# Conv stage and MLP as one block: the MLP's first tiles run inside the last conv batch's steps

## The chip, the cores and the metric

One NeuronCore of a Trainium2 chip. The metric is the device time of one launch in microseconds (us). Three runs of the kernel before are given, and one profiled execution.

## The reference, cut to what matters

Two layers over x of 4 batches by 512 tokens by 256 features. Layer 0 is attention and a mixture of 16 experts. Layer 1 is a gated convolution, an MLP and a mixture of two experts; this is the part that matters here:

```python
h = _rmsnorm(x)                                   # x is the modulated layernorm
x = x + _mamba_fallback(h, W_in, conv_w, conv_b, W_out)   # the gated conv
h = _rmsnorm(x)
m = jnp.einsum('bte,de->btd', jax.nn.relu(jnp.einsum('btd,ed->bte', h, W_mlp1)), W_mlp2)
return x + m
...
h = _layernorm(x, axis=-1) * (1 + cb) + sb
x = x + gb * _L1_ffn_ref(h, L1_ffn_gate_w, L1_ffn_w_gate, L1_ffn_w_up, L1_ffn_w_down)
```

## The kernel before, in words

The work is a row of blocks. Within a block each engine runs a program of its own, in an order that is written out, and engines wait for one another by semaphores; between blocks all engines wait for all. Two blocks touch the change: `gated_conv` (L1506) and `mlp_and_dispatch` (L1866).

Every float32 product is made of three matmuls of split numbers, (high, low), (low, high), (high, high), by the helper `split3` (L47, L48, L49). So a weight or an activation is first copied to a rounded high part (ScalarE) and then subtracted from itself to a low part (VectorE or GpSimd).

**The conv block** works on one batch of 512 tokens at a time, four batches (0 to 3), as a wavefront: `wavefront` takes pairs (lag, stage), goes through steps, and in each step calls every stage, in the order listed, on the batch step minus lag. Each engine has its own list (TensorE L1834, ScalarE L1694, VectorE L1779, GpSimd L1600). For one batch: combine layer 0's results, layernorm, RMS norm, transpose to columns (`columns(0)`), up-projection in four parts (`up`, PSUM banks 2 to 5), conv taps, silu and gate, down-projection in four parts (`down`, banks 6 and 7), eviction (`y_out`, L1610), transposes back (`rows`, L1831, banks 0 and 1), add to H (`add`, L1778), squares (L1680), variance (L1740), root on GpSimd (L1579), scaled rows (`rms(1)`, L1654), transposes (`columns(1)`, L1790), high part (`hi(1)`, L1691) and low part (`lo(1)`, L1755) into hT, which the MLP reads. In TensorE's steps the last ones are: step 5, down(0) and down(1) of batch 3, columns(1) of batch 2, down(2) and down(3) of batch 3, rows of batch 3; step 6, columns(1) of batch 3.

**The MLP block** takes for each batch eight tiles of 128 hidden features. Per tile: up (six matmuls of 512 columns into banks 0 to 3 in turn), relu to the high part on ScalarE (L1997), low part on VectorE (L2039), and down (six matmuls into banks 4 and 5), which TensorE runs two tiles behind. Banks 6 and 7 serve transposes and routing. The MLP's weights lie in eight tiles; at batch 0 each tile is split first, ScalarE L1991 and VectorE L2033, three ahead and then one per tile. Their load (L1481) is issued in the conv block already, into a buffer that layer 0's results had held. From batch 1 on, ScalarE and VectorE also split the experts' up weights (L2019, L2099), which SyncE's queue loads (L1959) once all low parts of the MLP's weights are done and after it has zeroed a DRAM table from a tile that GpSimd sets (L1951, L1964).

Memory on the left side is laid out in the order of allocation. The conv block's tiles are freed when it closes, and the tiles of the dispatch, of the up weights and of the MLP take the same places.

Of the kernel before, what the change touches and what calls it, by code (L numbers as in the profile page):

```python
# [13 lines left out]
P = 128  # L14
D = 256
# [25 lines left out]
def f32(ap):  # L41

    return ap.bitcast(F32)
# [1439 lines left out]

class ConvWeights:

    def __init__(self, k, c, w_in, w_out, taps, mlp_st):
# [5 lines left out]
        self.yg, self.gb = (mlp_st.rows, k.sb("c_yg", [P, L0_TOPK, TT, D], F32, c)), k.sb("c_gb", [P, B, D], F32, c)  # L1492
        self.tap = k.sb("c_tap", [P, IT, TAPS + 1], F32, c)
        self.rows = k.sb("c_rows", [P, B, 2 * D], F32, c)
        self.k, self.w_in, self.wo_in, self.rows_in = k, k.sem("c_w_in"), k.sem("c_wo_in"), k.sem("c_rows_in")
# [10 lines left out]
def gated_conv(k, d, H, hT, weights, mlp_w):  # L1506

    nc = k.nc
    with ExitStack() as c:
        n = lambda s: f"c_{s}"  # L1510
        wi_st, wo_st, tap, w_in, wo_in = weights.wi, weights.wo, weights.tap, weights.w_in, weights.wo_in
        wi_hi = k.sb(n("wi_hi"), [P, DM, 2 * INNER], F32R, c)
        wi_lo = k.sb(n("wi_lo"), [P, DM, 2 * INNER], F32R, c)
        wo_hi = k.sb(n("wo_hi"), [P, IT, D], F32R, c)
        wo_lo = k.sb(n("wo_lo"), [P, IT, D], F32R, c)
# [4 lines left out]
        ss, sq = k.sb(n("ss"), [P, 2, B, TT], F32, c), k.sb(n("sq"), [P, 2, TT, D], F32, c)  # L1520
        hn = k.sb(n("hn"), [P, 2, TT, D], F32, c)
        rhi, rlo = k.sb(n("rhi"), [P, 2, DM, T], F32R, c), k.sb(n("rlo"), [P, 2, DM, T], F32R, c)
        acc = k.sb(n("acc"), [P, 2, T], F32, c)
        sx, sz = k.sb(n("sx"), [P, 2, T], F32, c), k.sb(n("sz"), [P, 2, T], F32, c)
        yv, yf, yg = weights.yv, weights.yf, weights.yg
        yhi, ylo = k.sb(n("yhi"), [P, IT, T], F32R, c), k.sb(n("ylo"), [P, IT, T], F32R, c)
# [12 lines left out]
        block = c.enter_context(nc.Block())  # L1539

# [11 lines left out]
        @block.sync  # L1552
        def _(sp):
# [13 lines left out]
            mlp_w.load(sp)  # L1567

        @block.gpsimd
        def _(pool):  # L1570
# [23 lines left out]
            def split_y(e):  # L1594
                def stage(b):
# [5 lines left out]
                      (3, split_y(2)), (3, split_y(3)), (0, pair), (2, gate(0)), (1, root(IN)))  # L1601

        @block.scalar
        def _(act):
# [79 lines left out]
            def hi(i):  # L1684
                def stage(b):
                    for m in range(DM):
# [12 lines left out]
        @block.vector  # L1699
        def _(dve):  # L1700
            own = Chain(dve, own_dve)

            def combine(b):
# [837 lines left out]
```

## Time and profile before

| | us |
|---|---|
| runs: median of 3 (lowest, highest) | 1178.86 (1175.69, 1179.64) |
| profiled execution, device time | 1173.97 |
| its span | 1171.9 |
| TensorE, busy share of the span | 81% |
| VectorE, ScalarE, GpSimd | 63%, 56%, 39% |
| mean granted TensorE clock | 0.897 of full speed |

The profiled execution took 4.9 us less than the median of the three runs; 2.1 us of it lie outside the span. Times in the text are counted from the span's start. A granted clock of 1.00 is 2.4 GHz and 0.50 is 1.2 GHz; a stretch between is a mixture of the two.

### The profile page before, as it was taken

Reading aid. Unit: us, or ns where it says so; the run is one execution under the profiler, and the core shown is the slowest. Engines: PE = TensorE matmul, PEld = TensorE weight load, DVE = VectorE, ACT = ScalarE, POOL = GpSimd, SP = SyncE. Lnnn points to the kernel's source line nnn. Section 1 sums busy time; section 2 is a strip of 40 time slices with the busy share of each in tenths; the row PEclk is TensorE's granted clock in tenths of the full one; section 3 lists DMA queues with packets and bytes.
Section 4 is the critical chain, followed back from the end, with each engine's and each line's share of the span. In section 5 each row is a group of like instructions: output and inputs, shape, how many; then the busy total and the mean of one; then the engine's idle time right before and its main releaser. Section 6 shows DMA issues by size and latency. Waiting matters only on the chain. (4 is left out here: it accounts for less than half of the span.)

```text
span 1171.9 us, 21496 instructions
## 1 busy us (share of the span) xinstructions
PE 954.3 (81%) x5454; PEld 796.3 (68%) x5454; DVE 742.1 (63%) x1917; ACT 652.3 (56%) x1693; POOL 456.9 (39%) x637
## 2 busy tenths in 40 slices
PE   6671999999997767969999970689699974999992
PEld 2461788888886655758999960468487753888882
DVE  4870798999994676468555535996447773444444
ACT  3562898999993345458666642579533322333331
POOL 3373564666662177603444443576301121010000
PEclk9786898999998787979999995799899986999997
DMA  7066443343322522447343429310042203000004
GB/s 247 17 222 212 114 102 90 91 90 90 90 54 64 180 100 101 153 150 251 124 128 121 126 98 303 99 45 1 14 143 75 72 28 127 24 31 33 28 15 152
DMA packets 112107, 123.15 MB, mean 105 GB/s; under 512 B 46720, under 2 KB 85120, under 8 KB 111896
## 3 DMA queue, kind: packets, MB, share of 16 engines
q1 hardware_dynamic: 102584, 97.89, 28.4%
q0 software_dynamic: 8608, 23.20, 5.3%
q10 hardware_dynamic: 832, 1.05, 0.3%
q8 instruction: 40, 0.66, 0.2%
q14 instruction: 43, 0.35, 0.1%
HBM read 77.73 MB, written 44.35 MB: 104 GB/s over the span
## 5 line engine op out<-in xcount | busy, mean ns | idle before, releaser
L717 ACT ACTIVATE PR<-PS,nmax 128x128 f32<-128x128 f32 (+3 forms) x256 | 135.7, 553 | 9.7 <-DVE nmax L758 8.4
L758 DVE TENSOR_REDUCE nmax<-PS 128x1 f32<-128x128 f32 (+3 forms) x256 | 113.5, 481 | 42.4 <-PE PS L661 37.0
L635 POOL TENSOR_SCALAR PR<-PR,rinv 128x128 f32<-128x128 f32 (+3 forms) x256 | 132.3, 537 | 0.0
L1355 POOL DMA_INDIRECT r_results<-r_y,r_to x79 | 75.9, 961 | 111.8 <-DVE r_to L1410 76.8
L660 PE MATMUL PS<-K,Q 128*128 128x128 f32 (+3 forms) x256 | 84.6, 390 | 30.4 <-PEq L138 26.4
L766 DVE TENSOR_TENSOR PTlo<-PS,PThi 128x512 fp32r<-128x512 f32 (+1 forms) x192 | 103.0, 590 | 2.9 <-ACT PThi L727 2.9
L727 ACT ACTIVATE PThi<-PS 128x512 fp32r<-128x512 f32 (+1 forms) x192 | 97.0, 547 | 6.7 <-PE PS L673 6.7
L673 PE MATMUL PS<-ident,PR 128*128 128x128 f32 x640 | 86.7, 281 | 3.6 <-DVE PTlo L766 3.0
L689 PE MATMUL PS<-PThi,V 128*128 128x512 f32 (+3 forms) x256 | 85.3, 346 | 1.1 <-DVE PTlo L766 0.5
L2350 DVE TENSOR_TENSOR x_h<-PS,x_sg 128x256 f32<-128x256 f32 x68 | 28.9, 424 | 86.4 <-ACT x_sg L2304 86.4
L2304 ACT ACTIVATE x_sg<-PS 128x256 f32<-128x256 f32 x68 | 26.2, 385 | 95.2 <-PE PS L2444 95.2
L2279 POOL DMA_INDIRECT x_results<-x_y,x_to x17 | 16.4, 963 | 156.2 <-DVE x_to L2345 143.8
L689 PE MATMUL PS<-PTlo,V 128*128 128x512 f32 (+3 forms) x256 | 76.2, 323 | 0.0
L673 PEld LDWEIGHTS PS<-ident,PR 128*128 128x128 f32 x640 | 69.6, 143 | 9.6 <-DVE PTlo L766 5.5
L949 POOL DMA_INDIRECT r_sorted<-o_hrow,o_slots x64 | 64.8, 1012 | 28.7 <-issue 18.7
L1399 DVE TENSOR_TENSOR r_xlo<-PS,r_xhi 128x256 fp32r<-128x256 f32 x79 | 33.4, 423 | 65.6 <-ACT r_xhi L1370 61.2
L660 PEld LDWEIGHTS PS<-K,Q 128*128 128x128 f32 x256 | 51.7, 206 | 32.8 <-issue 30.0
L2442 PE MATMUL PS<-r_wlo,r_xhi 128*128 x158 | 59.7, 378 | 2.5 <-issue 2.0
L1370 ACT ACTIVATE r_xhi<-PS 128x256 fp32r<-128x256 f32 x79 | 30.4, 385 | 56.1 <-PE PS L2444 54.0
L661 PE MATMUL PS<-maskb,identb 128*128 128x128 bf16 x256 | 60.8, 238 | 0.0
L717 ACT ACTIVATION_READ_ACCUMULATOR PR<-PS,nmax 128x1 f32 x256 | 58.7, 229 | 0.0
L2428 PE MATMUL PS<-x_w,x_hhi 128*128 (+1 forms) x136 | 57.2, 437 | 1.8 <-DVE x_hlo L2354 1.7
(374 smaller groups left out, 3067.8 us busy)
## 6 DMA issues: line engine op xcount, KB each, us to landing
r_xg<-r_sorted SPq DMA_DIRECT2D x79, 129.0 KB
r_wst<-in_routed SPq DMA_DIRECT2D x16, 608.0 KB, 5.3
K<-k_parts SPq DMA_DIRECT2D x120, 64.0 KB, 1.8
v_parts<-vp SPq DMA_DIRECT2D x4, 1024.0 KB, 7.5
V<-v_parts SPq DMA_DIRECT2D x64, 64.0 KB, 2.1
mlp_st<-r_results SPq DMA_DIRECT2D x8, 512.0 KB, 7.9
c_yg<-r_results SPq DMA_DIRECT2D x8, 512.0 KB
mlp_st<-in_up SPq DMA_DIRECT2D x8, 512.0 KB, 3.7
```

The costliest lines, as they stand in the source:

```text
L635: pool.tensor_scalar(PR[:, e % 4, i, 0:w], PR[:, e % 4, i, 0:w], rinv[:, e % 4, i:i + 1], 1.0, ALU.mult, ALU.mult).then_inc(norm_done, 1)
L660: pe.matmul(k.PS[:, i, 0:w], Q4[u][:, s // 2, P * i:P * i + P], K4[u][:, s, 0:w], start=True, stop=False)
L661: pe.matmul(k.PS[:, i, w - P:w], k.identb[:], k.maskb[:], start=False, stop=True).then_inc(s_ready, 1)
L673: ins = pe.transpose(k.PS[:, 4 + bank, at % 512:at % 512 + P], PR[:, (e - TRANS) % 4, i, P * j:P * j + P], k.ident[:])
L689: ins = pe.matmul(O[:, P * j:T], V4[u][:, j, s, :], pt[:, ge % 2, PT_AT[j]:PT_AT[j] + w], start=(s == 0 and j == 0 and part == 0), stop=(s ...
L717: act.activation(PR[:, e % 4, i, 0:w], k.PS[:, i, 0:w], ACT.Exp, bias=nmax[:, e % 4, i:i + 1], accum_out=rsum[:, e % 4, i:i + 1]).then_inc ...
L727: act.activation(PThi[:, e % 2, at:at + w], k.PS[:, 4 + n, 0:w], ACT.Copy).then_inc(hi_done, 1)
L758: dve.tensor_reduce(nmax[:, e % 4, i:i + 1], k.PS[:, i, 0:P * (i + 1)], AX_X, ALU.max, negate=True).then_inc(max_done, 1)
L766: dve.tensor_tensor(PTlo[:, (e - LO) % 2, at:at + w], k.PS[:, 4 + n, 0:w], f32(PThi[:, (e - LO) % 2, at:at + w]), ALU.subtract).then_inc(l ...
L949: pool.indirect_dma_start(out=d.sorted, out_offset=bass.IndirectOffsetOnAxis(ap=slots[:, b * TT + t, choice:choice + 1], axis=0), in_=hrow ...
L1355: pool.indirect_dma_start(out=d.results, out_offset=bass.IndirectOffsetOnAxis(ap=to[:, i % TO_LANES:i % TO_LANES + 1], axis=0), in_=y[:, i ...
L2442: pe.matmul(out, x_hi, w_lo, start=first, stop=False)
```

## The change

Five parts.

1. There is one block. `gated_conv` no longer opens one, but returns its engine programs; `mlp_and_dispatch` writes its own as generators, which yield after every tile, and the conv programs take each a generator and advance it where the order says. After the last conv stage each engine runs its generator to the end.
2. On TensorE, four turns of the MLP (up 0; up 1; up 2 and down 0; up 3 and down 1) come in step 6 ahead of columns(1) of batch 3.
3. On ScalarE, weight tiles 0 to 3 are split in step 5 after silu_x(2) of batch 3, and tiles 4 to 7 at the end of step 5; relu tile 0 comes after y_out of batch 3, tile 1 after the squares of batch 3, tiles 2 and 3 after rms(1) of batch 3.
4. On VectorE, the low parts of all eight weight tiles come in a row at the end of step 6, after lo(1) of batch 2 and ahead of add of batch 3; low tiles 0 and 1 come after that add, then the variance of batch 3, low tiles 2 and 3, and lo(1) of batch 3.
5. The banks are renamed (tiles in 2 to 5, results in 6 and 7, transposes and routing in 0 and 1), the conv tiles are allocated in another order, so that the MLP's weight tiles fall on tiles that are free early, and waits on conv semaphores are added. SyncE and GpSimd run their whole conv part first, then wait for the last up-projection, then run the MLP's part.

```diff
@@ gated_conv, allocation order
-        wi_hi = k.sb(n("wi_hi"), [P, DM, 2 * INNER], F32R, c)
-        wi_lo = k.sb(n("wi_lo"), [P, DM, 2 * INNER], F32R, c)
         wo_hi = k.sb(n("wo_hi"), [P, IT, D], F32R, c)
         wo_lo = k.sb(n("wo_lo"), [P, IT, D], F32R, c)
+        sq = k.sb(n("sq"), [P, 2, TT, D], F32, c)
+        hn = k.sb(n("hn"), [P, 2, TT, D], F32, c)
...
+        weights.early(c)
+        wi_hi = k.sb(n("wi_hi"), [P, DM, 2 * INNER], F32R, c)
+        wi_lo = k.sb(n("wi_lo"), [P, DM, 2 * INNER], F32R, c)
...
@@ ScalarE
-            wavefront((2, first_tap(1)), (4, hi(1)), (1, squares(0)), (2, silu_x(0)), (3, y_out), (2, silu_z(1)), (2, split_y(0)), (2, silu_x(1)),
+            def go_on(n):
+                def stage(b):
+                    if b == B - 1:
+                        for _ in range(n):
+                            next(mlp)
+                return stage
+            wavefront((2, first_tap(1)), (4, hi(1)), (1, squares(0)), (2, silu_x(0)), (3, y_out), (3, go_on(1)), (2, silu_z(1)), (2, split_y(0)), (2, silu_x(1)),
                       (1, rms(0)), (2, first_tap(2)), (2, split_y(1)), (2, silu_z(2)), (2, first_tap(3)), (1, hi(0)), (1, split_out_weights), (2, silu_x(2)),
-                      (3, squares(1)), (2, split_y(2)), (2, silu_z(3)), (0, split_weights), (0, normalize), (2, silu_x(3)), (1, first_tap(0)),
-                      (3, rms(1)), (2, split_y(3)), (1, silu_z(0)))
+                      (2, go_on(1)), (3, squares(1)), (3, go_on(1)), (2, split_y(2)), (2, silu_z(3)), (0, split_weights), (0, normalize), (2, silu_x(3)), (1, first_tap(0)),
+                      (3, rms(1)), (3, go_on(2)), (2, split_y(3)), (2, go_on(1)), (1, silu_z(0)))
+            for _ in mlp:
+                pass
@@ VectorE
-            wavefront((4, add), (3, conv(2)), (1, stats_of), (2, lo(0)), (1, shift), (3, conv(3)), (4, rms_var(1)), (1, modulate),
-                      (2, conv(0)), (4, lo(1)), (2, conv(1)), (1, rms_var(0)), (1, split_weights), (0, combine))
+            wavefront((4, add), (4, go_on(2)), (3, conv(2)), (1, stats_of), (2, lo(0)), (1, shift), (3, conv(3)), (4, rms_var(1)), (4, go_on(2)),
+                      (1, modulate), (2, conv(0)), (4, lo(1)), (2, conv(1)), (1, rms_var(0)), (1, split_weights), (0, combine), (3, go_on(1)))
@@ TensorE
-            wavefront((2, down(0)), (2, down(1)), (1, up(0)), (1, up(1)), (3, columns(1)), (2, down(2)), (2, down(3)), (1, up(2)),
+            def go_on(b):
+                if b == B - 1:
+                    for _ in range(4):
+                        next(mlp)
+            wavefront((2, down(0)), (2, down(1)), (1, up(0)), (1, up(1)), (3, go_on), (3, columns(1)), (2, down(2)), (2, down(3)), (1, up(2)),
                       (2, rows), (1, up(3)), (0, columns(0)))
@@ mlp_and_dispatch
+        TILE, RESULT = (lambda i: k.PS[:, 2 + i % 4, :]), (lambda m: k.PS[:, 6 + m, :])
+        SIDE = lambda g: k.PS[:, g, :]
@@ its ScalarE program
-                split_weights(b, i, split)
...
+            act.wait_ge(conv.combined, B)
+            for half in range(2):
+                for i in range(half * MLP_T // 2, (half + 1) * MLP_T // 2):
+                    split(i)
+                yield
@@ its VectorE program
+            dve.wait_ge(conv.z_ready, B * IT)
+            for i in range(MLP_T):
+                split(i)
+            yield
@@ its TensorE program
                 if b == 0:
                     pe.wait_ge(wlo_done, i + 1)
+                    pe.wait_ge(conv.conv_done, B * IT)
+                    pe.wait_ge(conv.sz_done, B * IT)
+                if i == 0:
+                    pe.wait_ge(conv.hT_done, (b + 1) * DM)
@@ its SyncE and GpSimd programs
+            sp.wait_ge(conv.z_ready, B * IT)
             load_rows(0)
...
+            pool.wait_ge(conv.z_ready, B * IT)
             pool.memset(zero[:, 0:D + 1], 0.0).then_inc(zero_set, 1)
```

## Rows read from the trace of the kernel before

**Rows 1.** Busy time of each engine in three stretches around the seam

```profile
core 0: us, PE busy (x) PEld busy (x) DVE busy (x) ACT busy (x) POOL busy (x), PEclk, DMA share, GB/s
826.50:846.00 19.50, 8.35 (x37) 5.45 (x36) 4.92 (x10) 11.56 (x29) 6.47 (x11) 0.80 0.01 3
846.00:870.70 24.70, 24.70 (x97) 20.17 (x97) 12.02 (x17) 7.65 (x14) 0.00 (x0) 0.88 0.53 164
870.70:955.00 84.30, 79.58 (x389) 64.37 (x387) 57.86 (x129) 31.72 (x50) 10.99 (x11) 1.00 0.20 60
```

**Rows 2.** TensorE's timeline at the seam: start, us, line, what [idle before, releaser]

```profile
828.41 1.87 PE L1790 MATMUL PS<-ident,c_hn 128*128 128x128 f32 x8 [1.85 <-ACT c_hn L1654]
830.51 0.50 PE L47 MATMUL PS<-c_ylo,c_wo_hi 128*128 128x512 f32 x1 [0.23 <-POOL c_ylo L1598]
...
834.83 1.07 PE L1831 MATMUL PS<-ident,c_yf 128*128 128x128 f32 x8 [1.27 <-ACT c_yf L1610]
840.50 2.44 PE L1790 MATMUL PS<-ident,c_hn 128*128 128x128 f32 x8 [4.60 <-ACT c_hn L1654]
846.00 0.79 PE L47 MATMUL PS<-hT,m_whi 128*128 128x512 f32 x1 [3.07 <-DVE m_wlo L2033]
```

**Rows 3.** ScalarE's timeline at the seam

```profile
827.77 1.69 ACT L1654 ACTIVATE c_hn<-H,c_rs 128x256 f32<-128x256 f32 x4
...
833.60 1.09 ACT L1610 ACTIVATE c_yf<-PS 128x512 f32<-128x512 f32 x2 [2.64 <-PE PS L49]
...
839.85 1.71 ACT L1654 ACTIVATE c_hn<-H,c_rs 128x256 f32<-128x256 f32 x4 [1.32 <-POOL c_rs L1579]
...
844.60 1.67 ACT L1991 ACTIVATE m_whi<-mlp_st 128x512 fp32r<-128x512 f32 x3 [1.02 <-PEq L1509]
```

**Rows 4.** VectorE's timeline at the seam

```profile
830.51 1.29 DVE L1755 TENSOR_TENSOR hT<-PS,hT 128x512 fp32r<-128x512 f32 x2 [3.96 <-ACT hT L1691]
835.50 1.29 DVE L1778 TENSOR_TENSOR H<-PS,H 128x512 f32<-128x512 f32 x2 [3.70 <-PE PS L1831]
838.56 0.17 DVE L1740 TENSOR_SCALAR c_var<-c_ss 128x4 f32<-128x4 f32 x1 [1.77 <-ACT c_sq L1680]
...
845.26 1.89 DVE L2033 TENSOR_TENSOR m_wlo<-mlp_st,m_whi 128x512 fp32r<-128x512 f32 x3 [0.96 <-ACT m_whi L1991]
849.60 0.69 DVE L2039 SCALAR_TENSOR_TENSOR m_lo<-PS,m_hi 128x512 fp32r<-128x512 f32 x1 [2.45 <-ACT m_hi L1997]
```

**Rows 5.** GpSimd's timeline: the root of batch 3

```profile
838.81 1.01 POOL L1579 TENSOR_TENSOR c_rs<-c_var,mhalf 128x4 f32<-128x4 f32 x1 [7.10 <-DVE c_var L1740]
```

**Rows 6.** TensorE's timeline: first matmul of up 4, batch 0, and of up 0, batch 1

```profile
857.10 0.39 PE L47 MATMUL PS<-hT,m_whi 128*128 128x512 f32 x1
...
870.70 0.39 PE L47 MATMUL PS<-hT,m_whi 128*128 128x512 f32 x1
```

**Rows 7.** Short stretches around two falls of the clock (columns as in rows 1)

```profile
756.70:758.90 2.20, 0.06 (x2) 0.05 (x1) 2.13 (x3) 2.20 (x5) 1.47 (x1) 1.00 0.10 9
758.90:761.00 2.10, 2.10 (x6) 1.14 (x6) 2.06 (x6) 1.11 (x2) 0.24 (x1) 0.72 0.82 237
...
836.00:840.50 4.50, 0.00 (x0) 0.03 (x1) 0.96 (x3) 2.35 (x10) 1.01 (x1) 0.76 0.00 0
...
849.00:852.00 3.00, 3.00 (x8) 2.32 (x8) 1.29 (x2) 1.56 (x3) 0.00 (x0) 0.50 0.00 0
```

**Rows 8.** The up weights' path: SyncE's issue, ScalarE's first use, landing times of DMA issues

```profile
860.60 42.54 SPq L1959 DMA_DIRECT2D mlp_st<-in_up  x6
...
872.75 1.05 ACT L2019 ACTIVATE u_hi<-mlp_st 128x1024 fp32r<-128x1024 f32 x1
...
mlp_st<-in_up SPq DMA_DIRECT2D x8, 512.0 KB, 3.7
d_sorted<-m_h SPq DMA_DIRECT2D x1, 2193.0 KB, 11.4
```

**Rows 9.** VectorE's timeline: the last combine of the conv block

```profile
778.39 2.21 DVE L1715 TENSOR_TENSOR X<-X,c_yg 128x1024 f32<-128x1024 f32 x1
```

More of the change, by code:

```diff
@@ L1 @@
+from collections import namedtuple
 from contextlib import ExitStack
@@ L1567, in _, with gpsimd @@
             mlp_w.load(sp)
-        @block.gpsimd
-        def _(pool):
+            for _ in mlp:
+                pass
+        def gpsimd(pool, mlp):
             def pair(b):
@@ L1601, in _, with scalar @@
                       (3, split_y(2)), (3, split_y(3)), (0, pair), (2, gate(0)), (1, root(IN)))
-        @block.scalar
-        def _(act):
+            for _ in mlp:
+                pass
+        def scalar(act, mlp):
             def y_out(b):
@@ L1778, in add, with go_on, stage, tensor @@
                     dve.tensor_tensor(x, k.PS[:, g, :].rearrange("p (t d) -> p t d", t=2), x, ALU.add).then_inc(h_added, 1)
-            wavefront((4, add), (3, conv(2)), (1, stats_of), (2, lo(0)), (1, shift), (3, conv(3)), (4, rms_var(1)), (1, modulate),
-                      (2, conv(0)), (4, lo(1)), (2, conv(1)), (1, rms_var(0)), (1, split_weights), (0, combine))
-        @block.tensor
-        def _(pe):
+            def go_on(n):
+                def stage(b):
+                    if b == B - 1:
+                        for _ in range(n):
+                            next(mlp)
+                return stage
+            wavefront((4, add), (4, go_on(2)), (3, conv(2)), (1, stats_of), (2, lo(0)), (1, shift), (3, conv(3)), (4, rms_var(1)), (4, go_on(2)),
+                      (1, modulate), (2, conv(0)), (4, lo(1)), (2, conv(1)), (1, rms_var(0)), (1, split_weights), (0, combine), (3, go_on(1)))
+            for _ in mlp:
+                pass
+        def tensor(pe, mlp):
             def columns(i):
@@ L1863, in __init__, with mlp_and_dispatch @@
         self.done = k.sem("u_done")
-def mlp_and_dispatch(k, H, hT, weights, gate_w, d, up_w, up_d):
+def mlp_and_dispatch(k, conv, H, hT, weights, gate_w, d, up_w, up_d):
     nc = k.nc
@@ L1918, in interleave @@
                             stage(b - back)
-        def split_weights(b, i, split):
-            if b == 0:
-                for j in range(0 if i == 0 else i + 2, min(i + 3, MLP_T)):
-                    split(j)
+                    yield
         def up_part(at, stage):
@@ L1936, in up_tiles, with sync @@
             return ust[:, j % 2, :], up_w.hi[:, j // L1_CHUNKS, cols], up_w.lo[:, j // L1_CHUNKS, cols]
-        @block.sync
-        def _(sp):
+        def sync(sp):
             def load_rows(b):
@@ L1985, in _, with scalar @@
             wavefront((0, root), (0, scatter))
-        @block.scalar
-        def _(act):
+            yield
+        def scalar(act):
             def split(i):
@@ L2160, in rows @@
                     pe.wait_ge(slots_done, b)
+                else:
+                    pe.wait_ge(conv.hT_done, B * DM)
                 for g in range(2):
@@ L2196, in ranks, with _ @@
                     pe.matmul(total, k.onesb[:], d.count[:, NT - 1:NT], start=True, stop=True).then_inc(t_ready, 1)
-            interleave(up, (2, 2, ranks), (1, 3, rows), (1, 6, columns), (2, 0, gate),
-                       *((0, i + 2, down(i)) for i in range(MLP_T - 2)), (0, 7, down(MLP_T - 2)), (0, 7, down(MLP_T - 1)))
+            yield from interleave(up, (2, 2, ranks), (1, 3, rows), (1, 6, columns), (2, 0, gate),
+                                  *((0, i + 2, down(i)) for i in range(MLP_T - 2)), (0, 7, down(MLP_T - 2)), (0, 7, down(MLP_T - 1)))
+        block = c.enter_context(nc.Block())
+        @block.sync
+        def _(sp):
+            conv.sync(sp, sync(sp))
+        @block.gpsimd
+        def _(pool):
+            conv.gpsimd(pool, gpsimd(pool))
+        @block.scalar
+        def _(act):
+            conv.scalar(act, scalar(act))
+        @block.vector
+        def _(dve):
+            conv.vector(dve, vector(dve))
+        @block.tensor
+        def _(pe):
+            conv.tensor(pe, tensor(pe))
 def sorted_experts(k, d, up_w, down_d, out):
```

88 lines of the change are left out of this document (48 added, 40 removed).

## The prediction

> **What bounds the kernel now.** The busy time by stretches was read first, then each engine's timeline at the seam, then the clock. In 19.5 us around the seam TensorE is busy for 8.35 us and no other engine is full either, while in the MLP's batches 1 to 3 TensorE is busy for 79.6 of 84.3 us at a clock of 1.00 [rows 1]. So the MLP is bound by TensorE, and the seam by a chain of waits. TensorE's timeline shows the chain's gaps: 4.60 us until the scaled rows of batch 3, 3.07 us until the MLP's first low weights [rows 2]. The links between are add at 835.50, squares, variance at 838.56, root at 838.81, scaled rows at 839.85, transposes from 840.50 [rows 2 to 5]. Then high and low parts of hT, and the end of the block; ScalarE's first weight split comes at 844.60, 1.02 us late [rows 3], and up 0 starts at 846.00. The clock has fallen in the long gap (0.76 over 836 to 840.5) and is still 0.50 from 849 to 852 [rows 7]. Up 4 of batch 0 starts at 857.10 and batch 1 at 870.70 [rows 6]: 10 groups of six matmuls lie between, 1.36 us each, or 0.227 us a matmul.
>
> The measure of the change is thus when up 4 starts. The groups behind it are in the same order before and after, and ScalarE and VectorE need together some 1.3 us per tile (0.5 to 0.6 relu, 0.69 low part [rows 4]) where TensorE needs 2.7 us for an up and a down, so they keep pace.
>
> **Part by part, on a time axis of the kernel before.**
>
> *ScalarE, splits 0 to 3.* Three splits took 1.67 us [rows 3], 0.52 us each from start to start, so four take 2.1 us. ScalarE is full there: scaled rows of batch 2 start at 827.77 with no wait before them [rows 3]. All behind it moves by 2.1 us: these scaled rows to 829.9, columns(1) of batch 2 on TensorE from 828.41 to 830.5, down(2) of batch 3 from 830.51 to 832.6, y_out from 833.60 to 835.7, rows from 834.83 to 836.9, done at 838.0 [rows 2, 3]. This work has its waits met: the wait on all four combines is for one that ended at 780.6 [rows 9].
>
> *ScalarE, splits 4 to 7.* Another 2.1 us. They sit before hi(1) of batch 2 and so push lo(1) on VectorE from 830.51 by 4.2 us to 834.7, done at 836.0 [rows 4]. y_out, at 835.7, is not pushed further.
>
> *VectorE, the eight low weight parts.* Three took 1.89 us [rows 4], 0.61 us each from start to start: eight take 4.9 us, from 836.0 to 840.9. Add of batch 3 is queued behind them. Its data come at 835.50 + 2.1 = 837.6, but it starts at 840.9: 5.4 us later than before. Squares, variance, root, scaled rows and lo(1) all wait for it. This is the new bound of the seam.
>
> *TensorE meanwhile.* Up 0, 1 and 2 (4.1 us, banks free) run from 838.0 to 842.1. Down 0 needs low tile 0, which is behind add: 840.9 + 1.3 + 0.6 = 842.8. Down 0 and up 3 then run to 845.6, and down 1 to 847.1 once low tile 1 is there (below).
>
> *The chain of batch 3.* Before, from add's start to the scaled rows' start is 839.85 - 835.50 = 4.35 us [rows 3, 4]. Now relu tile 1 on ScalarE (0.5) and low tile 1 on VectorE (0.7) stand between the squares and the variance: 5.55 us. Scaled rows start at 840.9 + 5.55 = 846.5 and take 1.7 us [rows 3], to 848.2. The last five transposes, at the half rate 0.3 us apart (2.44 us for eight [rows 2]) and at the full rate about 0.12 (an estimate from 1.07 us for eight with the last one's own length in it [rows 2]), end at 848.9. Columns(1) is queued ahead of up 4, so up 4 starts at 848.9.
>
> *Edits at nothing.* The block's end (under 1 us [rows 3]) is in the old chain and goes with it. The renamed banks have the same number of turns. hi(1) and lo(1) of batch 3 and relu tiles 2 and 3 are covered by down 2 and up 5 (2.7 us); without that cover they would cost up to 1.7 us. On SyncE's queue nothing stands between the MLP weights' load and the new wait but that wait, and it is met when the last up-projection ends, which TensorE runs ahead of its gap at 826.56. GpSimd's memsets stand behind the root of batch 3, now near 846.5, so the zero fill of the table is issued near 846.9 and the up weights' loads right behind it, against 860.60 before [rows 8]. Taken one after another, 11.4 us for the fill and 3.7 us for the first load [rows 8] land at 862.0; ScalarE first needs it at 872.75 - 8.2 = 864.5 [rows 8]. Covered by 2.5 us at this pessimistic price.
>
> **Sum.** 857.10 - 848.9 = 8.2 us earlier, and all later work moves along, since batches 1 to 3 wait for nothing outside. The profiled execution's 1173.97 becomes 1165.8. It stood 4.9 us below the median of the runs; against that median, 1178.86, the forecast is 1170.7.
>
> **Bounds of what no row shows.** If VectorE's row of splits did not delay add (its earliest, 837.6), TensorE alone would bind: 838.0 + 6 groups of 1.37 us + 0.8 for the transposes is 847.0, a gain of 10.1 us. If the clock is low through the seam, the lower end is below. I stay with 8.2, since each link was seen at nearly that length.
>
> **The clock, for and against.** TensorE is now without work from 826.56 (828.41 less 1.85 [rows 2]) to 830.5, 3.9 us, then has transposes, and waits again until 832.6. In the trace a stretch of 2.2 us almost without work was followed by a fall from 1.00 to 0.72 in the next 2.1 us [rows 7], and 4.5 us by 0.76 within it [rows 7]; so a fall near 830 is more likely than not. After 846.00 the engine worked steadily and was at 0.50 until about 852 [rows 7]. If it is low to 839 it hides: down(2) and down(3), 12 matmuls at 0.43 us in place of 0.23, end 2.4 us later and rows near 840.8, still ahead of add's 840.9. Low until 845, nine or ten matmuls of the MLP are slow too and the gain is about 4.5 to 5; until 850 about 2. The Trainium skill, page "TensorE: Matmul & The Clock Gate", section "HAM oscillation — how this bites in real kernels", says that waits between short bursts can throttle the engine at each burst anew; by that rule the seam, which still has waits in it, would stay at half rate beyond one fall. The rows after 852 hold 1.00 through three batches [rows 1], so I give it the small chance below.
>
> **Rivals.**
> - *A low clock well into the MLP's first tiles* (until 845 to 850). For it: the new gap at 826.6 and the second at 830 to 832.6. Against: from 838 on TensorE has work almost without a break. Gain 2 to 5 us: 1174 to 1177.
> - *The gain is given back at the up weights.* If fill and loads land later than 864.5, ScalarE, which takes all in order, stops at L2019 with relu tile 0 done and tile 1 behind it. Each us later gives one back; all is gone at 872.7, 26 us after the issue, where my price is 15. For it: fill and loads now start together. Result 1171 to 1179.
> - *The change does not do what it says.* Were any of the added waits on a semaphore of the end of the conv part, up 0 would stay behind it. But the waits name the last conv taps, the last silu_z (which ScalarE runs ahead of the scaled rows at 827.77 [rows 3]), and batch 0's hT; none is late. Then 1178.9; I give it 1%.
> - *Slower: the half rate holds through the whole first batch.* The waits for low tile 0, low tile 1 and the scaled rows, about 0.7, 0.2 and 1 us, keep the clock at 1.2 GHz. Price: each further us at 0.50 costs about half a us. The gain is gone near 854, and 96 matmuls at 0.427 us in place of 0.227 would cost 19 us less the 2.8 us that the old kernel paid from 846 to 852: a loss of about 8 us, 1187.
>
> **Chances.** The forecast (1168.5 to 1172.5) 0.70; low clock until 845 or 850 0.15, two thirds of it a gain above 3.5 us; up weights late 0.07; nothing done 0.01; slower 0.07. About 0.3%, 3.5 us, is what a measurement of this kernel can tell from no change. So faster 0.80, same 0.13, slower 0.07. The range: low end, the gain of 10.1 us and 2 to 3 us for the scatter of the three runs, 1166.0; high end, the low clock to 850, 1176.8.
>
> **What would show it.** Right: up 0 near 838, ahead of columns(1) of batch 3; eight L2033 in a row before the last L1778, which starts near 841; up 4 near 849; batch 1 near 862.5; the span shorter by 8 us and every stage from batch 1 on of the same length. Wrong: a clock of 0.50 beyond 843; an idle time before L2019 or L1997 in batch 1 put down to a DMA; up 4 after 855; an MLP batch 1 to 3 longer than 28 us; or a conv stage before 823 that has changed at all, since nothing but places in memory is different there.

## The result and the profile after

| | median, us | lowest to highest | executions |
|---|---|---|---|
| changed kernel | 1164.43 | 1160.24 to 1168.03 | 4 |
| kernel before, on the same chip | 1177.28 | 1173.41 to 1179.64 | 4 |

The ratio is 0.9893 with a 95% interval of [0.9847, 0.9938]: faster by 1.1%, clear of the noise. The forecast was 1170.7 with a range from 1166.0 to 1176.8, so the result lies 6.3 us below the forecast and 1.6 us below the range. The profiled execution took 1168.03 us with a span of 1166.2.

The stretches of the changed kernel come first, to be held against [rows 1] and [rows 7]. Columns: from:to, length, busy time of PE, PEld, DVE, ACT, POOL with instructions, granted clock, DMA share, GB/s.

```profile
827.80:831.80 4.00, 0.00 (x0) 0.02 (x1) 0.17 (x1) 4.00 (x14) 1.46 (x2) 0.92 0.30 39
831.80:834.90 3.10, 3.09 (x10) 2.29 (x11) 0.00 (x0) 3.10 (x8) 3.10 (x3) 0.50 0.00 0
834.90:838.40 3.50, 3.50 (x10) 2.73 (x9) 2.42 (x5) 1.53 (x4) 0.19 (x1) 0.56 0.01 2
838.40:841.50 3.10, 1.83 (x13) 1.36 (x12) 3.10 (x7) 1.08 (x2) 0.00 (x0) 1.00 0.01 1
841.50:850.10 8.60, 8.60 (x44) 7.22 (x43) 3.60 (x7) 5.46 (x17) 1.65 (x7) 1.00 0.44 102
850.10:863.69 13.59, 13.59 (x61) 11.21 (x61) 7.16 (x10) 3.37 (x6) 0.00 (x0) 1.00 0.74 208
863.69:946.20 82.51, 77.92 (x377) 62.90 (x375) 57.85 (x128) 30.51 (x49) 10.97 (x11) 1.00 0.19 61
```

Before, TensorE did nothing for 4.60 us ahead of the last transposes and for 3.07 us ahead of the MLP's first tile [rows 2]; now it is full from 841.50 to 863.69. The clock fell in the gap that the change opened (0.92, then 0.50 and 0.56) and was back at 1.00 by 838.4; before, it was at 0.50 in the MLP's first tiles [rows 7], whose first 14 matmuls took 6.07 us (846.00 to 852.07); in the changed kernel they take 3.27. Next TensorE's timeline, against [rows 2] and [rows 6].

```profile
831.81 2.44 PE L1820 MATMUL PS<-ident,c_hn 128*128 128x128 f32 x8 [4.05 <-ACT c_hn L1668]
...
840.09 1.07 PE L1861 MATMUL PS<-ident,c_yf 128*128 128x128 f32 x8 [1.27 <-ACT c_yf L1624]
840.91 0.48 PE L48 MATMUL PS<-hT,m_whi 128*128 128x512 f32 x1
...
849.17 1.03 PE L1820 MATMUL PS<-ident,c_hn 128*128 128x128 f32 x8
849.96 0.48 PE L48 MATMUL PS<-hT,m_whi 128*128 128x512 f32 x1
...
863.69 0.39 PE L48 MATMUL PS<-hT,m_whi 128*128 128x512 f32 x1
```

Up 0 (840.91) follows the rows of batch 3 at once, and up 4 (849.96) follows columns(1) at once; neither has an idle time before it. ScalarE and VectorE, against [rows 3] and [rows 4]:

```profile
825.44 0.63 ACT L1677 ACTIVATE c_sx<-c_acc 128x512 f32<-128x512 f32 x1 [0.18 <-DVE c_acc L1790]
825.98 2.18 ACT L2027 ACTIVATE m_whi<-mlp_st 128x512 fp32r<-128x512 f32 x4
...
831.17 1.70 ACT L1668 ACTIVATE c_hn<-H,c_rs 128x256 f32<-128x256 f32 x4
...
833.29 2.18 ACT L2027 ACTIVATE m_whi<-mlp_st 128x512 fp32r<-128x512 f32 x4
...
847.43 1.71 ACT L1668 ACTIVATE c_hn<-H,c_rs 128x256 f32<-128x256 f32 x4 [1.92 <-POOL c_rs L1592]
...
865.75 1.05 ACT L2054 ACTIVATE u_hi<-mlp_st 128x1024 fp32r<-128x1024 f32 x1
```

```profile
835.99 1.29 DVE L1778 TENSOR_TENSOR hT<-PS,hT 128x512 fp32r<-128x512 f32 x2 [6.03 <-ACT hT L1705]
837.19 4.89 DVE L2072 TENSOR_TENSOR m_wlo<-mlp_st,m_whi 128x512 fp32r<-128x512 f32 x8
842.00 1.28 DVE L1801 TENSOR_TENSOR H<-PS,H 128x512 f32<-128x512 f32 x2
```

The row of eight low weights and the add right behind it without an idle time are what was forecast. For the up weights' path [rows 8], SyncE's issues and their landings (KB each, median us from issue to landing):

```profile
847.72 0.37 SPq L1986 DMA_DIRECT2D d_sorted<-m_h  x1
...
d_sorted<-m_h SPq DMA_DIRECT2D x1, 2193.0 KB, 10.8
mlp_st<-in_up SPq DMA_DIRECT2D x3, 512.0 KB, 10.4
```

Beside the fill, the first three loads take 10.4 us instead of 3.7, yet the first split of them on ScalarE (L2054, 865.75) waits for nothing.

**A measure for the seam.** Starting points drift by several us between executions, so all traces below are measured from the start of silu_x(2) of batch 3 on ScalarE (825.44 here, 824.12 before) to the first up matmul of batch 1 (863.69; before 870.70 [rows 6]). That is 46.58 us before and 38.25 after: 8.33 us less, where 8.2 was forecast. The seam is right and the total is not, so the experiments ask both what makes the seam's gain and where the other 4 us or so came from.

### The profile page after: what moved, and what is told of

It reads as the page before. It is cut to its first block and busy times, and to the rows that moved or that the text cites. A ratio compares the mean times of both kernels' runs of the same rounds, so it can differ in the third digit from the quotient of the medians.

```text
span 1166.2 us, 21505 instructions
## 1 busy us (share of the span) xinstructions
PE 951.9 (82%) x5454; PEld 795.4 (68%) x5454; DVE 742.0 (64%) x1917; ACT 650.6 (56%) x1693; POOL 454.6 (39%) x637
## 3 DMA queue, kind: packets, MB, share of 16 engines
q10 hardware_dynamic: 832, 1.05, 0.3%
```

## The experiments

Four series ran, each with fresh runs of the kernel before on its chip (medians 1175.81, 1173.27, 1173.83 and 1175.3, of 29, 11, 23 and 11 executions; all 74 together 1174.61). Ratios are against those. Offsets, written +x, count from silu_x(2) as above.

### Copies: how far the clock itself can be trusted

`null_before` and `null_before2` are the kernel before, `after_again`, `after_third` and `after_fourth` the changed kernel, without an edit.

> The kernel before against itself, unchanged. Both theories expect a ratio of 1 within its interval. What it measures is the scatter: how far two medians of a handful of runs of one kernel lie apart (the four runs known span 1173.4 to 1179.6), and how long each stretch of the trace is in a second execution. If stretches outside the seam differ by 1 us or more between two executions of this same kernel, the differences of that size between before and after outside the seam mean nothing.

> The kernel before once more, unchanged, for a third trace of it. silu_x of part 2, batch 3 starts at 824.1 and 828.8 in the two traces so far, and between 817.7 and 825.4 in the eight of kernels with the new order, of which 1.1 us are explained. If the rest is scatter between executions, this trace has a value between 819 and 829, with the difference in attention (227.9 to 233.4 us so far) and the experts; if something of the new kernels shortens the early stages, it is at 824 or above again.

> The changed kernel, once more, with more rounds. Measure: the seam, from the start of silu_x of part 2, batch 3, on ScalarE to the first up matmul of batch 1; 46.6 us in the trace before, 38.3 us in the trace after. Theory A (the change acts at the seam alone, and the first comparison's 12.9 us is 8.3 us and scatter): ratio near 0.993, 7 to 10 us; seam 38.3 again. Theory B (the new places in memory or the moved transfers also shorten other stages): ratio near 0.989, 12 to 14 us, and the stretches before 731 or after batch 1 of the MLP shorter than in the kernel before by 3 us or more in all.

> The changed kernel a third time, beside the others on the same chip. Theory A (sum of stages: 8.3 us at the seam, 0.9 at the conv block's start, 0.2 to 0.3 in the last conv batch): ratio 0.992, with an interval that may hold 0.990. Theory B (there is 3 us more elsewhere): 0.989 to 0.990.

> The changed kernel beside them. Seam 38.2 to 38.5 us as in three traces, ratio to the kernel before 0.990 to 0.993.

| kernel | median us (executions) | ratio [95%] | seam, us |
|---|---|---|---|
| null_before | 1174.4 (12) | 0.9988 [0.9971, 1.0006] | 45.13 |
| null_before2 | 1173.94 (12) | 1.0001 [0.9985, 1.0017] | 46.65 |
| after_again | 1164.01 (6) | 0.9901 [0.9876, 0.9926] | 38.00 |
| after_third | 1163.98 (5) | 0.9911 [0.9892, 0.993] | 38.00 |
| after_fourth | 1165.11 (6) | 0.9896 [0.9873, 0.9918] | 38.46 |

The 24 executions of the copies of before lie between 1170.83 and 1180.08, median 1173.94, mean 1174.5; the changed kernel's 21 have median 1164.40 and mean 1164.1. One execution scatters by about 2.2 us (standard deviation), far from the seam: in the three traces of before, attention from its first to its last Q matmul takes 230.35, 231.86 and 233.44 us, in the four of the changed kernel 227.92 to 231.75. The three runs on which the forecast was set, median 1178.86, stand 4.9 us above the copies' median. With the fresh runs and the first comparison's four there are 102 executions of the kernel before: 1170.35 to 1180.44, median 1174.6, mean 1174.9.

### one_block: the block's end alone

All turns of the MLP inside the conv stages are taken out; each generator runs whole after them.

```diff
@@ ScalarE
-            wavefront(... (3, y_out), (3, go_on(1)), (2, silu_z(1)), ...
+            wavefront(... (3, y_out), (2, silu_z(1)), ...
...
@@ VectorE
-            wavefront((4, add), (4, go_on(2)), (3, conv(2)), ...
+            wavefront((4, add), (3, conv(2)), ...
...
@@ TensorE
-            wavefront(... (1, up(1)), (3, go_on), (3, columns(1)), ...
+            wavefront(... (1, up(1)), (3, columns(1)), ...
```

> All of the change but the interleaving: one block, new memory layout, renamed banks, added waits; every turn of the MLP comes after the conv part on each engine. Theory A: only the end of the block goes, up 0 starts some 1.1 us earlier; seam 45.5 us, ratio 0.999. Theory B: the layout's share of the gain is here too, so 4 us or more beyond that, ratio 0.995 or less. A rival on the seam, that the end of the block was what cost, expects a seam near 40.

Measured: 1173.04 (12), ratio 0.9978 [0.9959, 0.9996], seam 45.89. The seam hardly differs from the 45.1 to 46.7 of the three traces of before, but the clock hides a part of it. In the stretch between the rows of batch 3 and up 0 the block's end can be seen by itself: 11.17 us in all three traces of before and in layout_only, 10.12 here, with a wait of 2.01 us ahead of up 0 in place of 3.07. So the block's end is worth 1.05 us, as expected; what hides it is that the rows came at +11.95, behind downs with six matmuls at half rate, where two of the three traces of before have them at +10.71 (the third at +12.07). One block is what makes the rest possible and one eighth of what saves the time. The ratio, 2.6 us with 2.1 either way, also holds the new places in memory (layout_only).

**The clock's share.** From up 0 on, the six traces without TensorE's turns differ only in how many of the MLP's first matmuls run at half rate. The first 14 took 6.07, 4.66 and 4.82 us in the three traces of before, 6.06 in layout_only, 5.23 here and 4.95 in splits_only; the rest up to batch 1 took 18.59 to 18.63 in all six. In all eleven traces with the turns they took 3.27 to 3.30. Before, the MLP starts behind waits of 4.60 and 3.07 us; with the turns it starts behind a wait of 1.27 us and a batch of transposes. So 1.4 to 2.8 us of the seam's gain are matmuls that run faster, and not idle time that is filled.

### splits_only: the weight splits moved, TensorE's turns left out

ScalarE's two turns of splits and VectorE's turn of eight stay where the change puts them; TensorE's four turns and the relu and low tiles go behind the conv part.

```diff
@@ ScalarE
- (3, y_out), (3, go_on(1)), (2, silu_z(1))
+ (3, y_out), (2, silu_z(1))
- (3, squares(1)), (3, go_on(1)), (2, split_y(2))
+ (3, squares(1)), (2, split_y(2))
- (3, rms(1)), (3, go_on(2)), (2, split_y(3))
+ (3, rms(1)), (2, split_y(3))
@@ VectorE
- (4, add), (4, go_on(2)), ...  (4, rms_var(1)), (4, go_on(2)),
+ (4, add), ...  (4, rms_var(1)),
@@ TensorE
- (1, up(1)), (3, go_on), (3, columns(1))
+ (1, up(1)), (3, columns(1))
```

> The changed kernel with the weight splits where the change puts them, but TensorE's first four turns and the relu and low tiles after the conv part. My theory of the prediction says that the splits alone cost: add of batch 3 starts 5.4 us later, columns(1) of batch 3 about 5 us later, up 0 near 848 instead of 846 and with the same slow clock, so a seam of 48 to 48.5 us, 1.5 to 2 us longer than before, ratio 1.001 to 1.002. The rival, that having the weights split ahead is what brings the gain, expects a seam of 43 us or less.

Measured: 1173.1 (10), ratio 0.9979 [0.9961, 0.9997], seam 47.18. A seam of 48 to 48.5 and a ratio above 1 had been expected; the seam is about 1 us shorter, and the ratio lies on the other side of 1, the new places in memory being in it too. TensorE's timeline:

```profile
842.37 2.44 PE L1820 MATMUL PS<-ident,c_hn 128*128 128x128 f32 x8 [6.96 <-ACT c_hn L1668]
844.45 0.77 PE L48 MATMUL PS<-hT,m_whi 128*128 128x512 f32 x1
```

VectorE's add of batch 3 is at +16.56, as in the changed kernel, so TensorE waits 6.96 us in place of 4.60 [rows 2] for the scaled rows. Up 0 follows the transposes without the 3.07 us wait of before; what the early splits save there is paid for ahead of the transposes. The last step from 47.18 to 38.25, 8.9 us, is therefore TensorE's four turns (with the relu and low tiles that feed them): they fill that wait, and with them the transposes of batch 3 (2.44 us here, 1.03 in the changed kernel) and the MLP's first 14 matmuls (4.95 and 3.27) run at full clock.

### warm_fill: is the clock's fall paid for?

Fourteen matmuls whose results nobody reads are put into TensorE's gap, behind down(1) of batch 3; nothing else changes.

```diff
+            def fill(b):
+                if b == B - 1:
+                    pe.wait_ge(conv_done, B * IT - 1)
+                    pe.wait_ge(sz_done, B * IT - 1)
+                    for _ in range(14):
+                        pe.matmul(k.PS[:, 2, :], wo_hi[:, 0, 0:P], yhi[:, 0, :], start=True, stop=True)
-            wavefront((2, down(0)), (2, down(1)), (1, up(0)), ...
+            wavefront((2, down(0)), (2, down(1)), (2, fill), (1, up(0)), ...
```

> The changed kernel with 14 matmuls of 512 columns into an idle PSUM bank (results unused) in TensorE's gap ahead of columns(1) of batch 2, where the changed kernel's trace has 4.05 us without work and the clock at 0.50 for the 12 matmuls of down(2) and down(3) of batch 3. Theory A (that fall hides behind VectorE's row of eight splits, as the prediction had it): down(2) and down(3) take 2.8 us instead of 4.3, rows of batch 3 start 1.5 to 2.4 us earlier, add still starts behind the splits, 16.6 us after silu_x(2); seam 38.3 us again, within 0.4. Rival (the clock is the bound there): seam 36 to 36.5.

Measured: 1164.09 (4), ratio 0.9922 [0.9895, 0.9949], seam 38.02. TensorE's timeline (silu_x(2) at 819.37), and then the stretches:

```profile
821.53 3.33 PE L1873 MATMUL PS<-c_yhi,c_wo_hi 128*128 128x512 f32 x14
...
832.16 1.07 PE L1861 MATMUL PS<-ident,c_yf 128*128 128x128 f32 x8 [1.27 <-ACT c_yf L1624]
```

```profile
822.00:826.00 4.00, 3.11 (x14) 2.19 (x12) 0.17 (x1) 4.00 (x15) 1.72 (x2) 1.00 0.11 23
826.00:829.00 3.00, 2.64 (x13) 1.78 (x13) 0.00 (x0) 3.00 (x8) 3.00 (x3) 1.00 0.01 3
```

The clock stays at 1.00 and the rows of batch 3 come at +12.79, not +14.65. The add is at +16.57 all the same, behind VectorE's row, and the seam with it. In the four traces of the changed kernel the clock over the 3 us from the transposes of batch 2 on is 0.50 to 0.53 each time, and 0.50 to 0.90 over the next 3 us; the rows come at +13.42 to +14.83 and the seam is 38.00 to 38.46. So the fall costs between nothing and 0.46 us: hidden nearly whole, as forecast.

### low_halves: VectorE's row cut in two

Low tiles 0 to 3 are split in a turn right after the variance of batch 2; tiles 4 to 7 only ahead of low tile 2.

```diff
- (4, rms_var(1)), (4, go_on(2)),
+ (4, rms_var(1)), (4, go_on(2)), (3, go_on(1)),
- (0, combine), (3, go_on(1)))
+ (0, combine))
...
-            for i in range(MLP_T):
+            for i in range(MLP_T // 2):
                 split(i)
             yield
...
+                if b == 0 and i == 2:
+                    for j in range(MLP_T // 2, MLP_T):
+                        split(j)
```

> The changed kernel with VectorE's row of eight low splits broken up: tiles 0 to 3 ahead of lo(1) of batch 2, where VectorE idles, tiles 4 to 7 after the variance of batch 3, ahead of low tile 2. The prediction's upper bound said 10.1 us instead of 8.2, a seam of 36.4, if this row did not delay add. With the slow clock seen at down(2) and down(3), my theory now is that TensorE binds at nearly the same length: rows of batch 3 at 14.7 us after silu_x(2), then 0.8 + 8.2 + 0.8 us of its own work: up 4 at 24.4, against 24.6 in the trace of the changed kernel. So add starts 1.2 us earlier and the seam is 38.0 to 38.3. The rival, VectorE's row alone is the bound, expects 36.4.

Measured: 1165.08 (4), ratio 0.993 [0.9902, 0.9958], seam 38.38. VectorE's timeline (silu_x(2) at 817.66):

```profile
822.09 3.58 DVE L2072 TENSOR_TENSOR m_wlo<-mlp_st,m_whi 128x512 fp32r<-128x512 f32 x4
...
833.08 1.29 DVE L1801 TENSOR_TENSOR H<-PS,H 128x512 f32<-128x512 f32 x2 [3.29 <-PE PS L1861]
...
838.29 2.49 DVE L2072 TENSOR_TENSOR m_wlo<-mlp_st,m_whi 128x512 fp32r<-128x512 f32 x4
```

The add is free of the row now: it waits 3.29 us for TensorE and is at +15.42, 1.1 us earlier. But the rows come at +14.76 and up 0 at +15.58, where the changed kernel has +14.65 and +15.47. TensorE holds the seam by itself here. The forecast's bound of 10.1 us for "TensorE alone" was wrong in just this: it had up 0 at 838.0, +13.9, with a clock that did not fall. The seam of 36.4 that this bound gives did not come.

### early_high_only and early_high: ScalarE's splits earlier

ScalarE splits the weight tiles in turns of three, three and two, after silu_x(0), after first_tap(2) and at the end of step 5, so that less of it stands ahead of the scaled rows of batch 2. In `early_high` the edit of low_halves is in too.

```diff
-            for half in range(2):
-                for i in range(half * MLP_T // 2, (half + 1) * MLP_T // 2):
+            for first, last in ((0, 3), (3, 6), (6, MLP_T)):
+                for i in range(first, last):
...
- (2, silu_x(0)), (3, y_out),
+ (2, silu_x(0)), (2, go_on(1)), (3, y_out),
- (2, first_tap(2)), (2, split_y(1)),
+ (2, first_tap(2)), (2, go_on(1)), (2, split_y(1)),
- (2, go_on(1)), (3, squares(1)), (3, go_on(1)),
+ (3, squares(1)), (3, go_on(1)),
```

> The changed kernel with ScalarE's eight high splits moved into its idle times of step 5: three ahead of y_out of batch 2, three ahead of split_y(1) of batch 3, two at the end of the step; VectorE's row of eight as in the change. Theory A: everything of ScalarE after silu_x(2) is 2.1 us earlier, so TensorE's gap is 2 us instead of 4 and the clock need not fall; lo(1) of batch 2 ends 3.1 us earlier, and with it the row of eight and add. Seam 35.2 us, 3 us shorter than the changed kernel's, ratio 0.987 to 0.988. The rival, ScalarE's splits are hidden and cost nothing in the change, expects 38.3.

> Early high splits with VectorE's row of eight as in the change, a second time. In the first trace the clock had fallen by down(2) too, but it hid behind the row. Theory A: seam 35.3 again, median 2 to 4 us below the changed kernel's. Theory C: a seam between 35 and 37.

> Both moves: the high splits in ScalarE's idle times and the low splits in halves. Theory A: the conv tail is then as in the kernel before, add of batch 3 starts 11.5 us after silu_x(2), and TensorE alone binds from rows on: 10.7 + 0.8 + 8.2 + 0.8 = 20.5 us to up 4, seam 34.1, 12.5 us shorter than before and 4.2 shorter than the changed kernel's; ratio to the kernel before near 0.986. The rival that the first move takes all (VectorE's row costs nothing once ScalarE is early) expects the same seam as the run before this one.

Measured: early_high_only 1162.07 (4), ratio 0.9904 [0.9876, 0.9931], seam 35.07; again, as early_high_only2, 1163.31 (6), 0.9883 [0.9858, 0.9908], seam 35.28. The 35.2 that was worked out is met; a ratio of 0.987 to 0.988 had been expected, which both intervals just reach. early_high: 1164.78 (6), 0.9922 [0.9901, 0.9943], seam 36.62, where 34.1 and a ratio near 0.986 were expected. VectorE of early_high_only (silu_x(2) at 822.06):

```profile
830.69 4.90 DVE L2072 TENSOR_TENSOR m_wlo<-mlp_st,m_whi 128x512 fp32r<-128x512 f32 x8
835.50 1.28 DVE L1801 TENSOR_TENSOR H<-PS,H 128x512 f32<-128x512 f32 x2
```

and the stretch just after the transposes of batch 2 in early_high, when TensorE runs down(2) and down(3):

```profile
828.02:830.02 2.00, 1.36 (x4) 1.08 (x4) 0.68 (x2) 1.77 (x4) 1.88 (x2) 0.70 0.35 107
830.02:832.02 2.00, 2.00 (x6) 1.54 (x5) 0.60 (x2) 0.00 (x0) 0.00 (x0) 0.50 0.33 94
```

With VectorE's row whole, the add is at +13.44 and up 0 at +12.26; with the row cut, GpSimd's low parts beside VectorE's take 2.95 us in place of 2.51, the downs start at +7.10 in place of +6.39, and eight of their matmuls are slow in place of three or four, so up 0 is at +13.81 and decides. Whether the cut row or the execution made the slow clock last longer is not shown.

### warm_early: the filler on top of early_high

Eight of warm_fill's matmuls, unread as there, in the edit of early_high, run twice (warm_early2 is the same kernel).

```diff
+                    for _ in range(8):
+                        pe.matmul(k.PS[:, 2, :], wo_hi[:, 0, 0:P], yhi[:, 0, :], start=True, stop=True)
```

> High splits in ScalarE's idle times, low splits in halves, and 8 filler matmuls (results unused) in TensorE's gap. In the run without the filler the 12 matmuls of down(2) and down(3) ran at half rate and rows of batch 3 started at 13.0 us after silu_x(2) instead of 10.7, with TensorE the bound, seam 36.8. Theory A (once VectorE's row is out of the way, the fall of the clock is paid in full): rows at 11.4 us (0.7 us of lateness of down(2) stays, GpSimd slowed beside VectorE's splits), seam 11.4 + 0.8 + 8.2 + 0.8 + 13.65 = 34.9, ratio near 0.987. The rival, that the clock costs nothing here either, expects 36.8 again.

> The filler version (early high splits, low splits in halves, 8 filler matmuls) a second time. Theory A (what the seam shortens, the run shortens): seam 35 us again, median 2 to 4 us below the changed kernel's on the same chip. Theory C (the clock at the seam differs between executions, and the first trace was a lucky one): seam 36 to 38.5 in this trace, median within 1.5 us of the changed kernel's.

Measured: 1164.02 (6), 0.992 [0.9901, 0.9938], seam 35.02; and 1163.5 (6), 0.9894 [0.9869, 0.992], seam 36.62. The same kernel, the same stretch, first in warm_early and then in warm_early2:

```profile
829.94:831.94 2.00, 1.36 (x7) 1.07 (x7) 0.68 (x2) 1.78 (x4) 1.91 (x2) 1.00 0.37 109
831.94:833.94 2.00, 1.73 (x8) 1.10 (x6) 0.61 (x2) 0.23 (x1) 0.00 (x0) 1.00 0.32 92
```

```profile
827.50:829.50 2.00, 1.36 (x4) 1.10 (x4) 0.68 (x2) 1.77 (x4) 1.89 (x2) 0.70 0.38 105
829.50:831.50 2.00, 2.00 (x6) 1.55 (x5) 0.61 (x2) 0.00 (x0) 0.00 (x0) 0.50 0.40 96
```

The filler kept the clock in one execution and not in the other, and the 1.6 us between the two seams are the 1.6 between their rows of batch 3 (+11.39 and +12.98). So a filler of this size is no safe means, and one trace is no proof of a clock. Nor did the time follow the seam: warm_early's seam is 3 us shorter than that of after_third on the same chip, and their medians are 1164.02 and 1163.98, where a ratio near 0.987 had been expected. Its other five executions may have had the low clock; no trace of them is kept.

**What the eleven traces with TensorE's turns have in common.** Two chains end at batch 1. From up 0, TensorE has six groups, the transposes and ten more groups, 22.8 us at full clock. From the add of batch 3 the scaled rows, transposes and the same ten groups take 21.45 us. The seam is the later of the two in every trace:

| trace | up 0 + 22.8 | add + 21.45 | seam |
|---|---|---|---|
| changed kernel | 38.27 | 38.01 | 38.25 |
| after_again, after_third | 37.64, 37.04 | 38.01 | 38.00, 38.00 |
| after_fourth | 38.45 | 38.01 | 38.46 |
| warm_fill | 36.41 | 38.02 | 38.02 |
| low_halves | 38.38 | 36.87 | 38.38 |
| early_high_only, and again | 35.06, 35.27 | 34.89 | 35.07, 35.28 |
| early_high | 36.61 | 35.10 | 36.62 |
| warm_early, and again | 35.01, 36.60 | 33.51, 35.10 | 35.02, 36.62 |

In the four traces of the changed kernel TensorE's chain ends last in two (the first one among them) and VectorE's in two. The two sums are fitted to these traces; that two constants serve eleven of them is what speaks for them.

### layout_only: the new order of memory alone

The kernel before, with only the allocation order of the changed one.

```diff
@@ gated_conv, its tiles
-        wi_hi = k.sb(n("wi_hi"), [P, DM, 2 * INNER], F32R, c)
-        wi_lo = k.sb(n("wi_lo"), [P, DM, 2 * INNER], F32R, c)
         wo_hi = k.sb(n("wo_hi"), [P, IT, D], F32R, c)
         wo_lo = k.sb(n("wo_lo"), [P, IT, D], F32R, c)
...
+        yhi, ylo = k.sb(n("yhi"), [P, IT, T], F32R, c), k.sb(n("ylo"), [P, IT, T], F32R, c)
+        weights.early(c)
+        wi_hi = k.sb(n("wi_hi"), [P, DM, 2 * INNER], F32R, c)
+        wi_lo = k.sb(n("wi_lo"), [P, DM, 2 * INNER], F32R, c)
...
```

> The kernel before with the conv tiles allocated in the order of the change and nothing else. In every trace of a kernel with the new order the stretch from the first combine of the conv block to its first transposes is 22.0 us, in both of the kernel before 22.9: batch 1's results land 0.93 us earlier, GpSimd's sum of them starts at 11.7 instead of 12.65 us, and VectorE's first multiply of the modulation, which stretches while GpSimd runs, takes 2.35 instead of 3.27 us. Theory A (the places in memory alone do this): 22.0 us here too, seam 45.3 to 46.8 as before, ratio 0.999. The rival (something of the one block does it) expects 22.9. A second rival, that the layout shortens the attention or the experts too, expects a ratio of 0.997 or less.

Measured: 1172.87 (12), ratio 0.9999 [0.9981, 1.0018], seam 47.30, a little above the 45.3 to 46.8 expected: it has both the late rows (+11.48) and 14 slow matmuls. The ratio shows nothing, but a trace resolves the start of the conv stage: from the first combine to the first transposes of the conv stage it takes 21.99 us, the same as in the other thirteen traces with the new order (21.98 to 22.05), and 22.92, 22.95, 22.92 in the three with the old. GpSimd, then VectorE, in null_before (first combine at 712.41):

```profile
725.07 2.34 POOL L1574 TENSOR_TENSOR c_yg<-c_yg 128x1024 f32<-128x1024 f32 x1 [2.21 <-DMA c_yg<-r_results]
...
725.20 3.29 DVE L1732 TENSOR_TENSOR H<-H,c_rows 128x1024 f32<-128x1024 f32 x1 [2.14 <-ACT H L1645]
```

and in layout_only (first combine at 705.54):

```profile
717.24 2.34 POOL L1581 TENSOR_TENSOR c_yg<-c_yg 128x1024 f32<-128x1024 f32 x1 [1.25 <-DMA c_yg<-r_results]
...
718.33 2.33 DVE L1739 TENSOR_TENSOR H<-H,c_rows 128x1024 f32<-128x1024 f32 x1 [2.14 <-ACT H L1652]
```

Batch 1's results land 0.96 us sooner, so GpSimd's addition starts at 11.70 and not at 12.66 after the first combine, and covers less of VectorE's multiply, which the transposes wait for. The multiply has 1.08 us left when GpSimd ends, in both (3.29 less the 2.21 from 725.20 to 727.41; 2.33 less the 1.25 from 718.33 to 719.58), of 1.22 us that it takes alone: it made next to no progress before. The Trainium skill, page "SBUF — State Buffer", section "SBUF: two separate sides", has VectorE and GpSimd share a pair of ports; when a VectorE instruction has two inputs in SBUF, as this multiply has, and GpSimd's reads SBUF too, the one that starts first holds the pair for its whole length while the other stands still; by that rule these rows are what is to be expected. Why the data land sooner from other places in memory was not tried.

## Why the prediction missed

**Right.** The mechanism and its size at the seam. As offsets, forecast and measured: columns(1) of batch 2 +6.4 and +6.37; down(2) of batch 3 +8.5 and +8.46; add of batch 3 +16.8 and +16.56; add to scaled rows 5.55 us and 5.43; up 4 +24.8 and +24.52; gain 8.2 us and 8.33 in the first pair, 7.9 between the means of three traces (46.12) and four (38.18). The rows of batch 3, "near 840.8" under a low clock, +16.7, came at +14.65, since the clock was back at 838.4. The up weights' loads slowed each other as feared and were in time. The agreement of 8.33 with 8.2 to a tenth is partly luck, since three traces of before differ by 1.5 us with the number of slow matmuls.

**Half right: the bound.** VectorE's row, "the new bound of the seam", shares that place. The forecast gave TensorE waits of about 0.7 and 0.2 us for low tiles 0 and 1 and of 1 us for the scaled rows. But the low clock moved up 0 to +15.47 (warm_fill, at full clock, has it at +13.61, where +13.9 was forecast), and from there on TensorE waited for nothing: the transposes start at 849.17, right behind down 1, and the scaled rows are done at 849.14. After 838.4 no row shows half rate, so the rivals of a low clock in the MLP did not occur. The Trainium skill, page "TensorE: Matmul & The Clock Gate", section "HAM oscillation — how this bites in real kernels", was cited in the prediction for a throttle at each burst anew. Here the only further wait, 1.27 us ahead of the rows, brought no fall, so these traces neither bear the rule out nor refute it.

**Where it failed, first: the reference.** The step is "against that median, 1178.86, the forecast is 1170.7". The sum against the profiled execution, 1165.8, was 1.4 us off; the one that was handed on was 6.3 off. The text saw that the profiled execution stood 4.9 us below the median of three and took the median as the truer one. The 24 executions of copies put the kernel before at 1173.94, and all 102 on record at 1174.6: near the profiled execution, and 4.9 and 4.3 us below the median of the three runs. That the profiled execution stood so close to the middle was luck too; what could have been known is that three runs, 4 us apart among themselves, do not fix it. The range made it worse: its low end allowed "2 to 3 us for the scatter of the three runs" and only with the gain of 10.1 us at once.

**Second, a term missed.** Of the conv stage before 823 the prediction said "nothing but places in memory is different there", put that at nothing, and named a change there as a sign of being wrong. That sign came. The new places are worth 0.93 us at the start of the conv stage (layout_only), and the first and the third silu_x of batch 3 lie 0.2 us closer (9.05 to 8.83, and 8.85 in layout_only). Outside the span, 2.1 us became 1.8. Together with the seam: 7.9 + 0.93 + 0.2 + 0.3 = 9.3 us.

**How it closes.** 1178.86 - 8.2 = 1170.7 was 6.3 too high: 4.9 from the reference and 1.1 from the sum (1.4 of missed terms, less 0.3 by which the seam's mean is under 8.2); 0.3 is left. Against the median of all 102 executions it is 4.3 and 1.1, and 0.9 is left. The medians of the copies differ by 9.5 us, their means by 10.4 with about 1.3 us (95%) either way; with all 102 the medians differ by 10.2 and the means by 10.8, with 1.0 either way. The ratios of the single series, 0.9896 to 0.9911, put it at 10.4 to 12.2 us against their own runs of before, each with 2 to 3 us either way. So the times show some 1.5 us more than the traces' 9.3, at the edge of what they resolve; its cause is open. It does not lie behind the seam: from there to the end the span has 301.2 to 302.2 us before and 301.2 to 302.5 after, with batches 1 to 3 of the MLP at 82.24 to 82.33 in either kernel. Layer 0's experts (first to last transposes of their inputs) take 172.33 to 174.80, in no order. The seam itself starts at 824.12 to 828.75 in the three traces with the old memory order and at 817.66 to 825.44 in the fourteen with the new, 4.1 us earlier on average, of which 1.1 are found. The attention stretch averages 231.9 in three traces with the old memory order and 230.4 in fourteen with the new (227.92 to 231.96); the two overlap, layout_only's ratio shows no such gain, and it is left open.

**A version that beats both.** early_high_only takes 3.0 us off the seam of the changed kernel in two traces. Ten executions have median 1162.84 and mean 1162.4, against 1164.40 and 1164.1 for the changed kernel: 1.7 us, with 1.9 either way at 95%. It is faster than the kernel before beyond doubt; over the changed kernel the traces show it and the times do not yet, and warm_early, with as short a seam, was no faster than its neighbour.

## What to carry to other kernels

A chain of waits at a seam can be forecast from rows of the trace, here to some tenths of a us, if each engine's queue is walked in order; then the total hangs on the reference, so add the change to as many executions as there are, the profiled one among them, and widen the range by their scatter. Before an engine is relieved, write down when the other chain would end: here they ended within 0.3 us of each other in the first trace, and relieving VectorE alone or TensorE alone gave nothing. Compare a stretch that the clock doesn't touch before a small edit is called worthless: the block's end, 1.05 us, was lost in the seam's scatter. "Only places in memory" is not free: compare the stretches before the edit as well.

## What the runs showed of the hardware

- Executions of one kernel of 1.17 ms scatter over 10 us (1170.35 to 1180.44, 102 executions), and the attention stretch alone over 3.1 us.
- A gap of 4.05 us on TensorE was followed by 0.50 to 0.53 over the next 3 us in all four traces of the changed kernel, but by anything from 0.50 to 0.90 over the 3 us after those; with gaps of 0.46 and 0.64 us and transposes between, two executions of one kernel went two ways (1.00 in one, 0.70 and then 0.50 in the other).
- Behind waits of 4.60 and 3.07 us, the first 14 matmuls of 512 columns took 4.66, 4.82 and 6.07 us in three executions of one kernel; behind a wait of 1.27 us and eight transposes, 3.27 to 3.30 us in eleven traces.
- VectorE's four low parts took 3.58 us beside GpSimd's work and 2.49 without it (low_halves); a multiply of 128x1024 took 3.29, 2.33 or, beside no GpSimd work, 1.22 to 1.23 us.
- Loads of 512 KB that took 3.7 us took 10.4 beside a fill of 2193 KB, and the fill took 10.8 us beside them.
